# The last key's term as one product per output half, its values laid out in memory, and a projection in halves and passes

## The chip, the core and the metric

One NeuronCore of one Trainium2 chip. The metric is the device time of one execution in microseconds (us), the median over the runs shown. The profile is of one execution of its own.

## The reference

Sizes: x 64 x 32 x 512, context 64 x 257 x 512, 16 heads; weights as in the shapes below. Everything is float32.

```python
x = x + cross(layernorm(x), ctx)      # layernorm again with gamma, beta inside
    q = (xn @ w_q) -> 16 heads of 64;  k, v = split(ctx @ w_kv)
    attn = softmax(q * 64**-0.5 @ k.T)          # 32 queries x 257 keys
    out = ((attn @ v) @ w_out + b_out) * tanh(gate)
x = x + linear_attention(layernorm(x))          # W_Q, W_K, W_V
x = x + ffn(layernorm(x))                       # silu(gate) * up, hidden 1536
```

## The kernel before

Five engines run programs written out by hand, tied by semaphores: `wait_ge` holds the engine, `then_inc` counts. A value in float32 is kept for PE as a rounded high part and the rest (fp32r), and `three` multiplies high by high, low by high, high by low (L83 to L85). Some products are plain float32.

**Projection** (`project_queries`). Four blocks of 512 tokens, t = 0 to 3. DVE normalises twice (`norm_moments`, `norm_scale`), each time asking GpSimd (POOL) for a power; PE turns the result (L300), DVE applies gamma and beta (`affine`), ACT rounds it (`high_x`), DVE subtracts (`split_x`). PE forms eight outputs j of four chunks c, twelve products each. The weights come as eight pieces into a ring of six (`WeightSplit`): ACT rounds (L110), POOL subtracts (L230), and a slot is loaded again after that. ACT takes all eight pieces before `high_x`.

**Cross-attention** (`cross_attention`). 16 turns of four batches; the last turn is written apart. q is folded with the key weights once a turn (`fold_pair`, `low_fold`), so keys and values are the context itself. For batch b, PE forms four score tiles of 257 keys, DVE takes the maximum, ACT the exponential, POOL scales, DVE turns 32x32 blocks, SP's four DMAs exchange them between partitions (`exchange`), ACT and DVE split them (`high_probs`, `split_probs`), and PE multiplies with 256 of the context's rows in four chunks (`mix_chunk`), copied by DVE (`keep_mix`, L718). `out_half` multiplies the mix with the value weights: eight heads a half, two 64-column products of 128 columns at a time in plain float32 (L634). The 257th key is apart: its values v for all batches are computed once (`last_values`, ACT L930, a scratch array, `v_dram`) and loaded each turn into 16 rows of `last_v`; its weights go from `last_z` by a transpose and a product with a mask `own` into `last_p` (`keep_last`, L730 and L733), and one product per head adds the term (L641). ACT and DVE split each half (`high_out`, `low_out`), SP stores it. In the loop eight fold products and four score tiles of the next turn stand between the halves, in the last turn nothing.

Before the loop PE folds, scores batch 0 and computes v; SP waits for `v_stored` ahead of the loop's first turn.

## Time and profile before

| | |
|---|---|
| median of 3 runs | 1829.09 us (1827.91 to 1829.17) |
| profiled execution | 1831.52 us; span 1829.7 us, granted clock 0.994 |
| busy: PE, DVE, ACT, POOL | 98%, 60%, 36%, 30% |
| a turn of the loop | 62.9 us, 15 of them and the last |

A row of a timeline gives start, duration, engine, line, operation, out<-in, count, and in brackets the idle time before and what ended it. PE rows start when the one ahead is still draining: count from start to start. The granted clock is a share of 2.4 GHz, so 0.50 is 1.2 GHz.

### The profile page before, as it was taken

To read this page: it belongs to the slowest core of one execution; us is meant where nothing else is said; L and a number is where in the kernel's file an instruction comes from. 1 tells how busy PE (TensorE), PEld (TensorE's weight loads), DVE (VectorE), ACT (ScalarE), POOL (GpSimd) and SP (SyncE) were. 2 spreads that over 40 slices of the span, in tenths; PEclk is the share of its full clock that TensorE was granted. 3 is DMA by queue.
4 is the path that set the end of the run, shared out by engine and by line. 5 is a ranking of instruction groups with operands and counts; after the bars stand their busy time and mean duration, and the time that the engine had idled before them with its cause. 6 is when DMAs were issued, how large, how long until landed. Compare 5 with 4: busy or idle time off the path is not lost.

```text
span 1829.7 us, 38379 instructions
## 1 busy us (share of the span) xinstructions
PE 1794.3 (98%) x14608; PEld 1545.7 (84%) x14608; DVE 1104.6 (60%) x2271; ACT 666.8 (36%) x1356; POOL 557.9 (30%) x546
## 2 busy tenths in 40 slices
PE   5999999999999999999999999999999999999999
PEld 4888988998898899889988987788887878888887
DVE  6636566666756665666667566787888643333322
ACT  2245444545544454445445444311112411111111
POOL 3015434534444354345344444421121000000000
PEclk9999999999999999999999999999999999999999
DMA  7325444543554454445435538523440501010100
GB/s 254 127 97 145 123 109 125 139 133 90 146 137 116 114 150 123 107 127 140 133 90 145 137 105 237 160 78 96 126 139 13 180 6 69 1 69 0 46 1 23
DMA packets 236124, 199.23 MB, mean 109 GB/s; under 512 B 12896, under 2 KB 193376, under 8 KB 236064
## 3 DMA queue, kind: packets, MB, share of 16 engines
q1 hardware_dynamic: 231632, 189.74, 36.6%
q10 hardware_dynamic: 4432, 8.65, 1.3%
q8 instruction: 42, 0.69, 0.2%
q14 instruction: 18, 0.15, 0.0%
HBM read 130.98 MB, written 33.82 MB: 90 GB/s over the span
## 4 chain that ended last, share of the span: by engine, by line
PE 90%; DMA 1%; DVE 1%; SPq 0%; POOL 0%; issue 0%; ACT 0%; DVEq 0%; POOLq 0%; ACTq 0%
PE s_ps L83 25%; PE s_ps L84 24%; PE s_ps L85 24%; PE s_ps L579 7%; PE s_ps L634 6%; PE s_ps L641 1%; PE s_ps L1373 1%; PE s_ps L1387 1%; PE s_ps L1313 0%; PE s_ps L1398 0%; DMA a_xin<-x 0%; DMA a_m_xn<-x 0%; PE s_ps L588 0%; PE s_ps L1362 0%; DMA o_lo<-x_o_lo 0%
## 5 line engine op out<-in xcount | busy, mean ns | idle before, releaser
L83 PE MATMUL s_ps<-w_cT_hi,w_space_hi 128*128 128x258 f32 x1024 | 293.3, 286 | 0.2 <-DVE w_space_lo L725 0.2
L84 PE MATMUL s_ps<-w_cT_lo,w_space_hi 128*128 128x258 f32 x1024 | 289.9, 283 | 0.0
L85 PE MATMUL s_ps<-w_cT_hi,w_space_lo 128*128 128x258 f32 x1024 | 288.3, 282 | 0.0
L530 POOL TENSOR_TENSOR x_prob<-x_prob,x_share 128x256 f32<-128x256 f32 x256 | 156.0, 615 | 337.8 <-DVE x_share L692 329.9
L718 DVE COPY x_mix<-s_ps 128x512 f32<-128x512 f32 x256 | 174.5, 687 | 69.4 <-PE s_ps L85 67.0
L83 PE MATMUL s_ps<-x_pT_hi,x_cn_hi 128*128 128x512 f32 x512 | 206.3, 403 | 4.1 <-DVE x_mix L718 4.1
L850 ACT ACTIVATE x_prob<-s_ps,x_negmax 128x257 f32<-128x257 f32 x256 | 121.9, 476 | 240.9 <-DVE x_negmax L687 237.7
L85 PE MATMUL s_ps<-x_pT_hi,x_cn_lo 128*128 128x512 f32 x512 | 201.6, 394 | 0.0
L84 PE MATMUL s_ps<-x_pT_lo,x_cn_hi 128*128 128x512 f32 x512 | 200.9, 392 | 0.0
L83 PEld LDWEIGHTS s_ps<-w_cT_hi,w_space_hi 128*128 128x128 f32 x1024 | 193.4, 189 | 6.2 <-issue 3.8
L84 PEld LDWEIGHTS s_ps<-w_cT_lo,w_space_hi 128*128 128x128 f32 x1024 | 193.9, 189 | 0.7
L85 PEld LDWEIGHTS s_ps<-w_cT_hi,w_space_lo 128*128 128x128 f32 x1024 | 192.9, 188 | 0.0
L687 DVE TENSOR_REDUCE x_negmax<-s_ps 128x1 f32<-128x257 f32 x256 | 106.9, 418 | 125.2 <-PE s_ps L85 125.1
L725 DVE TENSOR_TENSOR w_space_lo<-s_ps,w_space_hi 128x512 fp32r<-128x512 f32 x256 | 160.4, 679 | 33.0 <-ACT w_space_hi L863 33.0
L519 POOL TENSOR_TENSOR w_cT_lo<-e_raw_T,w_cT_hi 128x1028 fp32r<-128x1028 f32 x64 | 141.5, 2211 | 126.9 <-ACT w_cT_hi L835 126.9
L524 POOL TENSOR_TENSOR x_cn_lo<-e_raw_n,x_cn_hi 128x1024 fp32r<-128x1024 f32 x64 | 153.0, 2391 | 73.8 <-ACT x_cn_hi L841 73.8
L863 ACT ACTIVATE w_space_hi<-s_ps 128x512 fp32r<-128x512 f32 x256 | 130.5, 615 | 33.0 <-PE s_ps L579 33.0
L634 PE MATMUL s_ps<-x_mix,e_wv 128*64 128x128 f32 x2048 | 138.3, 275 | 0.0
L579 PEld LDWEIGHTS s_ps<-e_q,e_wk 64*128 64x128 f32 x2048 | 118.1, 188 | 15.7 <-issue 13.3
L579 PE MATMUL s_ps<-e_q,e_wk 64*128 64x128 f32 x2048 | 127.2, 277 | 1.7 <-SPq L495 1.7
L634 PEld LDWEIGHTS s_ps<-x_mix,e_wv 128*64 128x64 f32 x2048 | 114.2, 137 | 11.3 <-DVE x_mix L718 8.9
L83 PEld LDWEIGHTS s_ps<-x_pT_hi,x_cn_hi 128*128 128x128 f32 x512 | 96.8, 189 | 26.9 <-issue 4.8
(204 smaller groups left out, 3504.7 us busy)
## 6 DMA issues: line engine op xcount, KB each, us to landing
e_raw_T<-ctx_T SPq DMA_DIRECT2D x64, 514.0 KB, 4.7
e_raw_n<-ctx_nat SPq DMA_DIRECT2D x64, 512.0 KB, 4.1
x_prob_T<-x_blocks SPq DMA_DIRECT2D x256, 128.0 KB, 2.7
q<-q_q ACTq DMA_DIRECT2D x16, 512.0 KB, 2.8
e_q<-q SPq DMA_DIRECT2D x16, 512.0 KB, 4.1
o_hi<-x_o_hi SPq DMA_DIRECT2D x32, 256.0 KB, 3.3
o_lo<-x_o_lo SPq DMA_DIRECT2D x32, 256.0 KB, 3.8
a_oT_hi<-o_hi SPq DMA_DIRECT2D x16, 512.0 KB, 4.3
```

What stands on the lines that cost most here:

```text
L83: pe.matmul(out, lhs[0], rhs[0], start=start, stop=False)
L84: pe.matmul(out, lhs[0], rhs[1], start=False, stop=False)
L85: return pe.matmul(out, lhs[1], rhs[0], start=False, stop=stop)
L519: pool.tensor_tensor(cT[b % 2][1][:, :, 0:SK], raw_T[:, :, :], f32(cT[b % 2][0][:, :, 0:SK]), ALU.subtract).then_inc(Tlo_done.sem, 1)
L524: pool.tensor_tensor(cn[b % 2][1][:, :, :], raw_n[:, :, :], f32(cn[b % 2][0][:, :, :]), ALU.subtract).then_inc(nlo_done.sem, 1)
L530: pool.tensor_tensor(prob[:, i, 0:KT * P], prob[:, i, 0:KT * P], share[:, i:i + 1].to_broadcast([P, KT * P]), ALU.mult)\
L579: mm = pe.matmul(ps[:, banks[h], c * P:(c + 1) * P], wk[r, j, c * P:(c + 1) * P], q[r, j, :], start=True, stop=True)
L634: pe.matmul(out[h], w_v[:, c, n * HE:(n + 1) * HE], mix[:, c, :, place(n)], start=c == 0, stop=False)
L718: dve.tensor_copy(mix[:, c, b, :], ps[:, M_BANK[c % 2], :]).then_inc(mix_kept.sem, 1)
L725: dve.tensor_tensor(lo, ps[:, fold_order(ahead, j)[0][h], :].rearrange("p (c n) -> p c n", n=SQ), f32(hi), ALU.subtract).then_inc(fold_lo. ...
L850: act.activation(prob[:, i, 0:SK], ps[:, S_BANK[i], 0:SK], ACT.Exp, bias=negmax[:, i:i + 1], accum_out=total[:, i:i + 1]).then_inc(exp_don ...
L863: act.activation(of_head(fold[0], 2 * j + h), ps[:, fold_order(ahead, j)[0][h], :].rearrange("p (c n) -> p c n", n=SQ), ACT.Copy)\
```

## The change

- **The last key.** Each row of the last key's weights and values is split in high and low; three columns (high, low, minus the high part's copy) are made for each batch and key. `last_rows`, a new input, is the mask: 16 columns of which row belongs to which column block, and one of signs. Each half has one 128x128 by 512 product in fp32r (L711 in the numbering of the change) ahead of its 64-column ones, with a spread of its own (`spread_last`); the second is made behind `low_out` of the first half.
- **The values.** ACT writes the rounded v twice, DVE makes the rest, ACT writes it; SP first fills `v_laid` with zeros from `last_v`, and then lays v out by eight DMAs of 16x24x64 (`spread_v`) and waits. A turn then loads 128x256 with one DMA in place of four.
- **The projection.** The norm goes in two halves of two tiles. The first block's first four outputs are formed in three passes: high by high, low weights, low x. ACT rounds x straight from PSUM. Five products of zeros (`WARM`) run at the start. The second block is turned ahead of j = 7, not 5. POOL splits one piece of weights between the norms, not two, and the rest after both halves.

On PE, in `out_half(0)` of the loop, before:

```order
L634 MATMUL s_ps<-x_mix,e_wv 64x128 [waits x_mix_kept]
L634 MATMUL s_ps<-x_mix,e_wv 64x128
L634 MATMUL s_ps<-x_mix,e_wv 64x128 [waits x_mix_kept]
L634 MATMUL s_ps<-x_mix,e_wv 64x128
L634 MATMUL s_ps<-x_mix,e_wv 64x128 [waits x_mix_kept]
L634 MATMUL s_ps<-x_mix,e_wv 64x128
L634 MATMUL s_ps<-x_mix,e_wv 64x128 [waits x_mix_kept]
L634 MATMUL s_ps<-x_mix,e_wv 64x128
L637 ISA
L638 REGISTER_ALU [waits x_v_loaded]
L641 MATMUL s_ps<-x_last_p,x_last_v 64x128 [waits x_last_kept]
L641 MATMUL s_ps<-x_last_p,x_last_v 64x128
```

and now:

```order
L709 REGISTER_ALU [waits x_v_loaded]
L710 REGISTER_ALU [waits x_mix_kept]
L711 MATMUL s_ps<-x_last_p,x_last_v 128x512 [waits x_last_kept]
L720 MATMUL s_ps<-x_mix,e_wv 64x128 x6
L720 MATMUL s_ps<-x_mix,e_wv 64x128 [waits x_mix_kept]
L720 MATMUL s_ps<-x_mix,e_wv 64x128 x25
```

The L641 products behind each block of eight are gone, and one of 512 columns stands ahead, with the waits for the values and the third chunk in front of it.

On DVE, from the third batch's last copy to the fold's fourth pair, before (`last_t` to `last_p` is `keep_last`), and now:

```order
L718 COPY x_mix<-s_ps 128x512 [waits x_mixed] x2
L730 STREAM_TRANSPOSE x_last_t<-x_last_z 128x128 [waits x_last_ready]
L732 ISA [waits x_last_turned]
L733 TENSOR_TENSOR x_last_p<-x_last_t,x_own 128x512 [waits x_o_ready]
L725 TENSOR_TENSOR w_space_lo<-s_ps,w_space_hi 128x16x32 [waits x_fold_hi]
L725 TENSOR_TENSOR w_space_lo<-s_ps,w_space_hi 128x16x32 [waits x_fold_hi]
L718 COPY x_mix<-s_ps 128x512 [waits x_mixed] x2
```

```order
L797 COPY x_mix<-s_ps 128x512 [waits x_mixed] x2
L809 STREAM_TRANSPOSE x_last_t<-x_last_z 128x64 [waits x_last_ready]
L812 CAST x_last_h<-x_last_t 128x64 [waits x_last_turned]
L814 SCALAR_TENSOR_TENSOR x_last_t<-x_last_t,x_own,x_last_h 128x64 [waits x_last_turned]
L817 ISA [waits x_last_turned]
L822 TENSOR_TENSOR x_last_p<-x_last_t,x_own 128x512 [waits x_o_ready]
L804 TENSOR_TENSOR w_space_lo<-s_ps,w_space_hi 128x16x32 [waits x_fold_hi]
```

Two operations and two waits came in. In the same turn, behind `low_out` (L829) and ahead of `low_fold(6)`, the second spread now stands:

```order
L829 TENSOR_TENSOR x_o_lo<-s_ps,x_o_hi 128x512 [waits x_o_hi_done]
L822 TENSOR_TENSOR x_last_p<-x_last_t,x_own 128x512
L802 REGISTER_ALU
L804 TENSOR_TENSOR w_space_lo<-s_ps,w_space_hi 128x16x32 [waits x_fold_hi]
L802 REGISTER_ALU
L804 TENSOR_TENSOR w_space_lo<-s_ps,w_space_hi 128x16x32 [waits x_fold_hi]
```

On POOL, at the start of the projection, before and now (L222 and L232 are the powers, L230 and L225 the split of weights):

```order
L222 TENSOR_TENSOR q_rstd<-q_shifted,q_power 128x4 [waits q_var_ready,q_power_set]
L230 TENSOR_TENSOR q_wq_lo<-q_raw,q_wq_hi 128x512 [waits q_w_hi_done,q_dve_chain]
L230 TENSOR_TENSOR q_wq_lo<-q_raw,q_wq_hi 128x512 [waits q_w_hi_done]
L222 TENSOR_TENSOR q_rstd<-q_shifted,q_power 128x4 [waits q_var_ready]
L230 TENSOR_TENSOR q_wq_lo<-q_raw,q_wq_hi 128x512 [waits q_w_hi_done,q_normed]
L230 TENSOR_TENSOR q_wq_lo<-q_raw,q_wq_hi 128x512 [waits q_w_hi_done] x5
```

```order
L232 TENSOR_TENSOR q_rstd<-q_shifted,q_power 128x2 [waits q_var_ready,q_power_set]
L232 TENSOR_TENSOR q_rstd<-q_shifted,q_power 128x2 [waits q_var_ready]
L225 TENSOR_TENSOR q_wq_lo<-q_raw,q_wq_hi 128x512 [waits q_w_hi_done]
L232 TENSOR_TENSOR q_rstd<-q_shifted,q_power 128x2 [waits q_var_ready] x2
L225 TENSOR_TENSOR q_wq_lo<-q_raw,q_wq_hi 128x512 [waits q_w_hi_done,q_normed]
L225 TENSOR_TENSOR q_wq_lo<-q_raw,q_wq_hi 128x512 [waits q_w_hi_done] x6
```

The second piece moved behind the powers and the wait for the norm.

The core of the diff:

```diff
+            def low_weights(numbers):
+                for n in numbers:
+                    pool.wait_ge(weights.hi_done, n + 1)
+                    pool.tensor_tensor(pieces[n][2], weights.raw[n % weights.RING][:, :], f32(pieces[n][1]),
+                                       ALU.subtract).then_inc(weights.lo_done, 1)
+
             for t in range(TURNS):
                 for k in range(2):
-                    pool.wait_ge(var_ready.sem, var_ready.at(t, k + 1))
-                    pool.tensor_tensor(rstd[:, :], shifted[:, :], power[:, :], ALU.pow).then_inc(rstd_done.sem, 1)
+                    for h, half in enumerate(HALVES):
+                        pool.wait_ge(var_ready.sem, var_ready.at(t, 2 * k + h + 1))
+                        pool.tensor_tensor(rstd[:, half], shifted[:, half], power[:, half], ALU.pow)\
+                            .then_inc(rstd_done.sem, 1)
                     if t == 0:
-                        if k == 0:
-                            pool.wait_ge(dve_chain, SCALED)
-                        else:
-                            pool.wait_ge(normed.sem, normed.at(0, 1))
-                        for n in range(2) if k == 0 else range(2, len(pieces)):
-                            pool.wait_ge(weights.hi_done, n + 1)
-                            pool.tensor_tensor(pieces[n][2], weights.raw[n % weights.RING][:, :], f32(pieces[n][1]),
-                                               ALU.subtract).then_inc(weights.lo_done, 1)
+                        if k == 1:
+                            pool.wait_ge(normed.sem, normed.at(0, 2))
+                        low_weights(range(1) if k == 0 else range(1, len(pieces)))
...
                     dve.wait_ge(x_loaded.sem, x_loaded.at(t, 16))
-                norm_moments(dve, chain, xin, stats, moments, shifted, TT, var_ready,
-                             x_first if t == 0 else None)
-                dve.wait_ge(rstd_done.sem, rstd_done.at(t, 1))
-                chain.step(norm_scale(dve, xn, xin, moments, rstd, TT))
-                norm_moments(dve, chain, xn, stats, moments, shifted, TT, var_ready)
-                dve.wait_ge(rstd_done.sem, rstd_done.at(t, 2))
-                norm_scale(dve, xn2, xn, moments, rstd, TT).then_inc(normed.sem, 1)
+                for half in HALVES:
+                    spread(xin, half)
+                for h, half in enumerate(HALVES):
+                    chain.step(scale(xn, xin, half, h + 1))
+                    spread(xn, half)
+                for h, half in enumerate(HALVES):
+                    scale(xn2, xn, half, h + 3).then_inc(normed.sem, 1)
...
                 for c in range(DC):
-                    act.wait_ge(affine_done.sem, affine_done.at(t, c + 1))
-                    act.activation(xT[t % 2][0][:, c, :], affine[:, c, :], ACT.Copy).then_inc(xhi_done.sem, 1)
-
+                    act.wait_ge(turned.sem, turned.at(t, c + 1))
+                    act.activation(xT[t % 2][0][:, c, :], ps[:, c, :], ACT.Identity, scale=g[:, c:c + 1],
+                                   bias=b[:, c:c + 1]).then_inc(xhi_done.sem, 1)
+
+            act.wait_ge(once, 48)
...
+            def first_products():
+
+                for part in range(2):
+                    for c in range(DC):
+                        if part == 0:
+                            pe.wait_ge(weights.hi_done, c + 1)
+                            pe.wait_ge(xhi_done.sem, xhi_done.at(0, c + 1))
+                        else:
+                            pe.wait_ge(weights.lo_done, c + 1)
+                        for j in range(4):
+                            pe.matmul(ps[:, 4 + j, :], wt[part][:, c, j * P:(j + 1) * P], xT[0][0][:, c, :],
+                                      start=part == 0 and c == 0, stop=False)
+                for j in range(4):
+                    for c in range(DC):
+                        if j == 0:
+                            pe.wait_ge(xlo_done.sem, xlo_done.at(0, c + 1))
+                        mm = pe.matmul(ps[:, 4 + j, :], wt[0][:, c, j * P:(j + 1) * P], xT[0][1][:, c, :],
+                                       start=False, stop=c == DC - 1)
+                    mm.then_inc(q_ready.sem, 1)
+
+            pe.wait_ge(zeroed, 1)
+            pe.wait_ge(var_ready.sem, var_ready.at(0, 2))
+            for _ in range(WARM):
+                pe.matmul(ps[:, 7, :], q[:, 0, 0:P], q[:, 0, :], start=True, stop=True)
             pe.wait_ge(once, 48)
-            turn_x(0)
+            turn_first()
+            first_products()
...
-    last_p = s.sb("last_p", [P, TILES, GB, SQ])
-    last_v = s.sb("last_v", [P, inner])
-    last_z, last_t = s.sb("last_z", [P, TILES, SQ]), s.sb("last_t", [P, TILES, SQ])
-    own = s.sb("own", [P, GB])
+    last_p = s.sb("last_p", [P, 2, PAIRS // 2, GB, SQ], F32R)
+    last_v = s.sb("last_v", [P, 2, P], F32R)
+    last_z, last_t = s.sb("last_z", [P, TILES, SQ // 2]), s.sb("last_t", [P, 2, SQ])
+    last_h = s.sb("last_h", [P, 2, SQ], F32R)
+    OWN = GB * PAIRS // 2
+    own = s.sb("own", [P, OWN + 1])
...
         def load_v(t):
             sp.wait_ge(o_ready.sem, o_ready.at(t, 0))
+            sp.dma_start(f32(last_v[:, :, :]), v_laid[bass.ds(t, 1), :, :].rearrange("t p (m n) -> p (t m) n", m=2))\
+                .then_inc(v_loaded.sem, 16)
+
+        def spread_v():
+
+            sp.wait_ge(v_cleared, 16)
+            sp.wait_ge(v_stored, 48)
+            src = v_dram.rearrange("(t b) k (m l g e) -> t (b k) m l g e", t=TURNS, m=2, l=2, g=HT)
+            dst = v_laid.rearrange("t p (m h e) -> t p m h e", m=2, h=2)
             for g in range(HT):
-                dst = last_v[g * SQ:g * SQ + GB, :].rearrange("b (i g e) -> b i g e", g=HT, e=HE)[:, :, g, :]
-                src = v_dram[bass.ds(t * GB, GB), :].rearrange("b (i g e) -> b i g e", g=HT, e=HE)[:, :, g, :]
-                sp.dma_start(dst, src).then_inc(v_loaded.sem, 16)
+                for l in range(2):
+                    at = g * SQ + l * SQ // 2
+                    sp.dma_start(dst[:, at:at + GB * PARTS, :, g % 2, :], src[:, :, :, l, g, :]).then_inc(v_spread, 16)
...
+        sp.dma_start(own[:, :], last_rows).then_inc(own_loaded, 16)
         sp.wait_ge(cleared, 1)
+        sp.dma_start(v_laid.rearrange("t p n -> p t n"),
+                     f32(last_v[:, :, :]).rearrange("p (t m) n -> p t (m n)", t=1).to_broadcast([P, TURNS, 2 * P]))\
+            .then_inc(v_cleared, 16)
...
-        sp.wait_ge(v_stored, 16)
+        spread_v()
+        sp.wait_ge(v_spread, 16 * 2 * HT)
...
-            pool.tensor_tensor(last_z[:, :, b % GB], prob[:, :, SK - 1], share[:, :], ALU.mult)\
+            at = b % GB * PARTS
+            pool.tensor_tensor(last_z[:, :, at:at + PARTS], prob[:, :, SK - 1:SK].to_broadcast([P, TILES, PARTS]),
+                               share[:, :].rearrange("p (i k) -> p i k", k=1).to_broadcast([P, TILES, PARTS]), ALU.mult)\
...
         def out_half(t, m):
+            if m == 0:
+                pe.wait_ge(v_loaded.sem, v_loaded.at(t, 16))
+                pe.wait_ge(mix_kept.sem, mix_kept.at(t, GB * DC - 1))
+            pe.wait_ge(last_kept.sem, last_kept.at(t, m + 1))
+            pe.matmul(ps[:, O_BANK[m], :], last_v[:, m, :], last_p[:, m, :, :, :].rearrange("p j b q -> p (j b q)"),
+                      start=True, stop=False)
             for j in range(4 * m, 4 * m + 4):
                 out = [ps[h * HE:(h + 1) * HE, O_BANK[m], j % 4 * P:(j % 4 + 1) * P] for h in range(2)]
                 for c in range(DC):
-                    if j == 0:
-                        pe.wait_ge(mix_kept.sem, mix_kept.at(t, (GB - 1) * DC + max(c + 1, DC - 1)))
+                    if j == 0 and c == DC - 1:
+                        pe.wait_ge(mix_kept.sem, mix_kept.at(t, GB * DC))
                     for h in range(2):
                         n = 2 * j + h
-                        pe.matmul(out[h], w_v[:, c, n * HE:(n + 1) * HE], mix[:, c, :, place(n)],
-                                  start=c == 0, stop=False)
-                if j == 0:
-                    pe.wait_ge(v_loaded.sem, v_loaded.at(t, 16 * HT))
-                    pe.wait_ge(last_kept.sem, last_kept.at(t, 1))
-                for h in range(2):
-                    n = 2 * j + h
-                    mm = pe.matmul(out[h], last_v[:, n * HE:(n + 1) * HE],
-                                   last_p[:, n // HT, :, :].rearrange("p b q -> p (b q)"), start=False, stop=True)
+                        mm = pe.matmul(out[h], w_v[:, c, n * HE:(n + 1) * HE], mix[:, c, :, place(n)],
+                                       start=False, stop=j == 4 * m + 3 and c == DC - 1)
...
         def keep_last(t):
             dve.wait_ge(last_ready.sem, last_ready.at(t, GB))
-            dve.transpose(last_t[:, :, :], last_z[:, :, :]).then_inc(last_turned.sem, 1)
+            dve.transpose(last_t[:, :, :], last_z[:, :, :].rearrange("p (m l) r -> p m (l r)", m=2))\
+                .then_inc(last_turned.sem, 1)
             dve.wait_ge(last_turned.sem, last_turned.at(t, 1))
+            dve.tensor_copy(last_h[:, :, :], last_t[:, :, :]).then_inc(last_turned.sem, 1)
+            dve.wait_ge(last_turned.sem, last_turned.at(t, 2))
+            dve.scalar_tensor_tensor(last_t[:, :, :], last_t[:, :, :], own[:, OWN:OWN + 1], f32(last_h[:, :, :]), ALU.mult,
+                                     ALU.add).then_inc(last_turned.sem, 1)
+            dve.wait_ge(last_turned.sem, last_turned.at(t, 3))
             dve.wait_ge(o_ready.sem, o_ready.at(t, 0))
-            dve.tensor_tensor(last_p[:, :, :, :],
-                              last_t[:, :, :].rearrange("p i (b q) -> p i b q", b=1).to_broadcast([P, TILES, GB, SQ]),
-                              own[:, :].rearrange("p (i b q) -> p i b q", i=1, q=1).to_broadcast([P, TILES, GB, SQ]),
+            spread_last(t, 0)
+
+        def spread_last(t, m):
+            shape = [P, OWN, SQ]
+            dve.tensor_tensor(last_p[:, m, :, :, :].rearrange("p j b q -> p (j b) q"),
+                              last_t[:, m, :].rearrange("p (x q) -> p x q", x=1).to_broadcast(shape),
+                              own[:, 0:OWN].rearrange("p (x q) -> p x q", q=1).to_broadcast(shape),
                               ALU.mult).then_inc(last_kept.sem, 1)
...
             low_out(t, 0)
+            spread_last(t, 1)
...
+        dve.wait_ge(own_loaded, 16)
+        dve.wait_ge(v_rounded, 1)
+        dve.tensor_tensor(all_last[1], ps[0:B, M_BANK[0]:M_BANK[0] + 2, :], f32(all_last[0]), ALU.subtract)\
+            .then_inc(v_copied, 1)
...
-        act.activation(all_last, ps[0:B, M_BANK[0]:M_BANK[0] + 2, :], ACT.Copy).then_inc(v_copied, 1)
+        act.activation(all_last[0], ps[0:B, M_BANK[0]:M_BANK[0] + 2, :], ACT.Copy).then_inc(v_rounded, 1)
+        act.wait_ge(v_rounded, 1)
+        for k in (0, 2):
+            act.dma_start(v_dram[:, k, :].rearrange("b (h n) -> b h n", h=2), f32(all_last[0])).then_inc(v_stored, 16)
         act.wait_ge(v_copied, 1)
-        act.dma_start(v_dram.rearrange("b (h n) -> b h n", h=2), all_last).then_inc(v_stored, 16)
+        act.dma_start(v_dram[:, 1, :].rearrange("b (h n) -> b h n", h=2), f32(all_last[1])).then_inc(v_stored, 16)
...
+    last_rows = np.zeros((4, 2, 16, 17), np.float32)
+    for g, l, b, k in itertools.product(range(4), range(2), range(4), range(3)):
+        last_rows[g, l, 3 * b + k, 4 * (2 * l + g // 2) + b] = -1 if k == 2 else 1
+        last_rows[g, l, 3 * b + k, 16] = -1 if k == 2 else 0
```

## Rows read from the trace of the kernel before

**Rows 1.** Busy shares on the page, part 1.

```profile
PE 1794.3 (98%) x14608; PEld 1545.7 (84%) x14608; DVE 1104.6 (60%) x2271; ACT 666.8 (36%) x1356; POOL 557.9 (30%) x546
```

**Rows 2.** PE timeline, output halves of two turns (start, us, engine, line, operation, count).

```profile
250.88 1.29 PE L634 MATMUL s_ps<-x_mix,e_wv 128*64 128x128 f32 x16
...
313.18 0.39 PE L84 MATMUL s_ps<-x_pT_lo,x_cn_hi 128*128 128x512 f32 x1
313.41 0.40 PE L85 MATMUL s_ps<-x_pT_hi,x_cn_lo 128*128 128x512 f32 x1
313.74 1.29 PE L634 MATMUL s_ps<-x_mix,e_wv 128*64 128x128 f32 x16
...
318.45 1.27 PE L579 MATMUL s_ps<-e_q,e_wk 64*128 64x128 f32 x18
...
326.37 1.09 PE L634 MATMUL s_ps<-x_mix,e_wv 128*64 128x128 f32 x16
327.30 0.39 PE L641 MATMUL s_ps<-x_last_p,x_last_v 128*64 128x128 f32 x4
327.51 1.04 PE L634 MATMUL s_ps<-x_mix,e_wv 128*64 128x128 f32 x16
...
330.89 0.39 PE L83 MATMUL s_ps<-w_cT_hi,w_space_hi 128*128 128x258 f32 x1
```

**Rows 3.** Weight loads (PEld) in the timeline of the first half.

```profile
314.59 0.20 PEld L634 LDWEIGHTS s_ps<-x_mix,e_wv 128*64 128x64 f32 x4 [0.22 <-DVE x_mix L718]
```

**Rows 4.** DVE timeline: a turn of the loop, and the last turn.

```profile
306.71 0.30 DVE L730 STREAM_TRANSPOSE x_last_t<-x_last_z 128x128 f32<-128x128 f32 x1
307.14 0.69 DVE L733 TENSOR_TENSOR x_last_p<-x_last_t,x_own 128x512 f32<-128x512 f32 x1
...
309.72 0.69 DVE L718 COPY x_mix<-s_ps 128x512 f32<-128x512 f32 x1 [0.69 <-PE s_ps L85]
...
320.29 2.48 DVE L725 TENSOR_TENSOR w_space_lo<-s_ps,w_space_hi 128x512 fp32r<-128x512 f32 x4 [0.40 <-ACT w_space_hi L863]
...
1124.51 1.47 DVE L733 TENSOR_TENSOR x_last_p<-x_last_t,x_own 128x512 f32<-128x512 f32 x1
```

**Rows 5.** Chain of waits behind the last turn's first half (start, us, what).

```profile
1136.95 0.61 ACT x_o_hi L877
```

**Rows 6.** Timeline of the loop's first turn: SP, ACT and PE.

```profile
146.91 3.35 SPq L435 DMA_DIRECT2D x_last_v<-v  x4
...
152.87 3.08 SPq L423 DMA_DIRECT2D x_prob_T<-x_blocks  x4
...
158.21 1.15 ACT L858 ACTIVATE x_pT_hi<-x_prob_T 128x512 fp32r<-128x512 f32 x2 [0.41 <-DMA x_prob_T<-x_blocks]
160.53 0.48 ACT L850 ACTIVATE x_prob<-s_ps,x_negmax 128x257 f32<-128x257 f32 x1 [1.17 <-DVE x_negmax L687]
...
162.32 0.28 PE L83 MATMUL s_ps<-w_cT_hi,w_space_hi 128*128 128x258 f32 x1
```

**Rows 7.** PE timeline of the last turn, around its longest idle time.

```profile
1123.76 0.76 PE L83 MATMUL s_ps<-x_pT_hi,x_cn_hi 128*128 128x512 f32 x1 [4.13 <-DVE x_mix L718]
...
1129.44 0.44 PE L84 MATMUL s_ps<-x_pT_lo,x_cn_hi 128*128 128x512 f32 x1
```

**Rows 8.** Stretch of 1127 to 1129 us (PE busy, granted clock, DMA share, GB/s).

```profile
1127.00:1129.00 2.00, 2.00 (x6) 0.50 0.04 16
```

**Rows 9.** Timeline of the projection's start: POOL, DVE, ACT and PE.

```profile
11.23 2.49 POOL L230 TENSOR_TENSOR q_wq_lo<-q_raw,q_wq_hi 128x512 fp32r<-128x512 f32 x2 [2.03 <-DVE q_xn L141]
...
15.40 1.91 DVE L141 TENSOR_SCALAR q_xn<-q_xn,q_moments,q_rstd 128x512 f32<-128x512 f32 x4 [1.13 <-POOL q_rstd L222]
16.74 0.63 ACT L110 ACTIVATE q_wq_hi<-q_raw 128x512 fp32r<-128x512 f32 x1 [1.12 <-DMA q_raw<-wq]
...
23.06 0.47 PE L83 MATMUL q_ps<-q_xT_hi,q_wq_hi 128*128 128x512 f32 x1 [2.32 <-DVE q_xT_lo L255]
...
42.33 0.48 PE L83 MATMUL q_ps<-q_xT_hi,q_wq_hi 128*128 128x512 f32 x1
```

93 lines of the change are left out of this document (61 added, 32 removed).

## The prediction

> **What bounds the kernel.** I read the page's busy shares first, then the PE timeline of one turn of the cross-attention loop, then what stands beside it. PE is busy for 98% of the span [rows 1]. Busy is a modelled number, so what I trust is the distance between starts: inside a turn one matmul starts after another with no gap that a release explains. A product of the 512-wide fp32r kind starts 0.23 us after the one ahead of it, and the output's second half runs 4.52 us from its first start at 326.37 to the next tile's at 330.89 [rows 2]. So a turn's length is the sum of PE's own starts, and instructions taken from PE there shorten the kernel as long as DVE, ACT, POOL and SP keep their lead. The time of a difference is made against the profiled execution: span 1829.7 us, 1831.52 us as timed; the median of the runs shown is 1829.09 us, 2.4 us under it. What a measurement of this kernel can tell from no change is about 0.2%, 3.7 us.
>
> **Part 1, the last key's product, steady turns.** Each half of the output holds four blocks of L641, x4 records each. One block takes 0.21 us, from 327.30 to the next start at 327.51 [rows 2]; by the half's 80 records in 4.52 us it would be 0.226. I take 0.22, so 0.87 us a half. In its place comes one product of 128x128 weights and 512 columns, fp32r, the kind with the pitch of 0.23. The second half so saves 0.87 - 0.23 = 0.64 us. The first half is longer today: 313.74 to 318.45 [rows 2], 4.71 against 4.52. The difference of 0.2 is a wait: PE's weight load stands idle for 0.22 us until DVE has copied the last mix chunk [rows 3]. The new product is put ahead of that wait and covers it. But it waits itself for the third chunk's copy, so its weights can't be loaded early, for which I add 0.1 us. The first half: 0.87 + 0.20 - 0.23 - 0.10 = 0.74. A turn saves 1.38 us; bounds are 0.92 (the product at twice its pitch in both halves) and 1.65 (no load delay, the block at 0.226, the product wholly inside the wait). Fifteen turns of the loop: **20.7 us**, 14 to 25.
>
> DVE's additions. In keep_last the transpose starts at 306.71, takes 0.30, and 0.13 later, at 307.14, the spread starts [rows 4]. Two operations of 64 columns come in between, each with such a wait behind it; the nearest row is that transpose of 128 columns, 0.43 with its wait. I take 0.24 apiece for the half width, 0.48 us. DVE is idle for 0.69 us before the copy at 309.72 [rows 4], which is the cover; with it gone each microsecond would reach the next mix chunk. The second spread (0.69 us, as L733 today) stands between low_out and low_fold 6, where DVE idles 0.40 us at 320.29 [rows 4]: it makes the low parts of the fold 0.29 late. PE needs the last of them for the third score tile, more than a microsecond behind. Nothing is charged, and this is rival C. POOL's last_z with three columns a key and the single load of last_v (SP issues one for four) have cover too: they are 0.2 us of POOL, and SP then waits for DVE's tiles anyway.
>
> **Part 2, the last turn.** There no fold and no scores stand between the halves, so PE's second half has to wait for the second spread, which DVE does behind ACT's high_out and its own low_out. ACT's copy is 0.61 [rows 5]; low_out is taken to cost what the spread does, 0.69 [rows 4], and the spread the same; with hand-overs 2.0 us from the first half's end, where now the second half follows at once. The halves themselves get shorter by 0.74 and 0.64, less 0.1 for the second's weight load. A loss of 2.0 - 0.74 - 0.54 = **0.7 us**, up to 1.5 if the spread meets POOL's weight work, where L733 once took 1.47 [rows 4]. The chain of waits behind it (POOL and DVE split weights) isn't shortened by what PE does.
>
> **Part 3, laying the values out, before the loop.** Today ACT writes v once, and SP is released by its landing at 146.91 [rows 6]. Now a third write follows, of what DVE leaves: DVE takes the rounded part off 64x1024 values in PSUM. Twice the 0.69 of a 512-wide operation is the upper end, 0.69 the lower; I take 1.2, so the third write lands at 148.1. Only then does SP issue eight scattered DMAs and wait for all of them, with the exchange of key block 1 queued behind. No row shows such a DMA. Nearest are the exchange's four: 3.08 us to issue, and the last landed when ACT was released at 158.21, 2.3 us behind the last issue [rows 6]. Eight at 0.77 and 2.3 make 8.4 us; if packets count (3072 rows against 1024), three times 3.08 and 2.3 make 11.5. I take 9.4, near the first because the queue was busy with issuing: spread at 157.5. With load_v and load_q ahead, the exchange starts at 158.6 instead of 152.87, 5.7 late. ACT's high_probs blocks the exps of block 2 behind it: today the third is over at 161.0 and PE needs it for the tile at 162.3 [rows 6], a lead of 1.3 us. PE stands for 5.7 - 1.3 = 4.4 us. A stand of that length has a second price: after 4.13 us idle in the last turn, thirteen matmuls took 5.68 us (0.44 each) [rows 7] with a granted clock of 0.50 [rows 8], the 1.2 GHz level, 2.7 us more than at 0.23. Together **7.1 us lost**; 0 if the spread lands by 151, 14 if it needs twice as long.
>
> The Trainium skill, page "DMA: Bandwidth & Descriptors", section Specifications, asks for at least 512 B a transfer, below which the engine reads, modifies and writes. The spread's rows are 256 B, so by that rule these DMAs would be the slower bound or worse, and the loss some 9 to 10 us; no row of this trace prices such a row alone.
>
> The zeroing of the laid-out array (2 MB) goes ahead of the loads of the keys. I charge nothing for it, and no row prices it: a load of keys that comes 3 us later delays only the first normalisation, whose tiles PE uses after the scores of a whole block.
>
> **Part 4, the projection.** The first matmul starts at 23.06 [rows 9], long after the transposes. What gates it now is the eighth piece of weights: ACT rounds all eight before it touches x, and the ring of six lets piece 8 load only when POOL has split two. Today POOL splits both at 11.23 to 13.72, between two norms, and ACT rounds the eighth at 16.74, 3.0 later [rows 9]. Held back, the second split stands behind both halves' norm. The norm itself ends at 17.3 now (15.40 + 1.91); with halves the waits for POOL's power are filled, 1.1 to 1.2 us each; I take 15.8. POOL splits by 17.1, the piece lands at 20.1, ACT is done with it at 20.8, x rounded straight from PSUM is there at 21.4. **So the matmuls start 1.7 us sooner, not more.** From there PE has 96 of them and one set of transposes: 96 x 0.227 + 1.9, plus the low clock for 2.7, ends at 47.8. Before: j 5 to 7 start at 42.33 [rows 9], and 36 x 0.227 end at 50.5. The gain is **2.7 us**; the passes need the low parts only at the 33rd matmul, so POOL and DVE, which share time there, are out of the way. Bounds: 0 (a wait for the second block of tokens, whose norm starts some 2.4 later than now), and 5.4 (the clock stays up, since five products of zeros run ahead).
>
> **Sum:** 20.7 - 0.7 - 7.1 + 2.7 = 15.6 us. Against its own time the profiled execution would be 1831.52 - 15.6 = 1815.9; from the median, 1829.09 - 15.6 = **1813.5 us**.
>
> **Rivals.**
> A, the spread is hidden: it lands while PE does blocks 0 and 1 and no stand of PE forms. For it: SP waits for DVE's tiles until 152.87. Against it: eight issues alone end at 154. It gives 15.6 + 7.1 = 22.7, 1806.4 us.
> B, the change doesn't do what it says: the new product costs what the old ones did. For it: the old blocks are two 64-column products side by side, and joining them fills rows with zeros, so no work need be saved. If it took 0.87, only the wait of 0.2 is won, 3.0 us, less 5.1 of the other parts: 1831.2, no change. Against it: products of the same types and size run at 0.23 [rows 2].
> C, DVE's extra 1.2 us a turn reach PE through the exchange of the next turn: 0.4 us a turn would be 6 us, 1819.5 us. Against it: 0.69 and 0.40 of idle time just there [rows 4].
> D, slower: SP is held by the spread. With X us from the third write's landing to the spread's, PE stands for X - 5.0, and has 22.7 to spare with 2.7 of them for the clock: the kernel is slower from X = 25 on, which is 130 ns a row on each of 16 engines, where the exchange's 1024 packets in 5.3 us [rows 6] make 83 with the latency in. At X = 35 it is 30 + 2.7 - 22.7 = 10 us slower, 1839.1 us. Rows of 256 B from memory to memory speak for it, the size of the factor against it.
>
> **Chances.** Forecast 0.60, A 0.17, C 0.14, B 0.04, D 0.03, else 0.02. The range takes in the forecast's bounds, A and most of C: 1804 to 1821 us. Faster by more than 0.2%: 0.92; within: 0.04; slower: 0.04.
>
> **What would show it.** Right: the distance from one turn's first half to the next, 62.86 us now (250.88 to 313.74) [rows 2], becomes 61.5; one idle row of PE of 4 to 5 us near 160, with the granted clock at 0.50 behind it; the first fp32r product near 21.4; PE idle for 2 us between the halves of the last turn. Wrong: turns of 62.5 or more (B or C, told apart by the new product's own distance), an idle time before the loop over 10 us, or none.

## The result and the profile after

The changed kernel takes 1818.53 us (median of 5 runs, 1817.80 to 1821.15), the kernel before 1829.09. The ratio is 0.9947, 95% interval [0.9936, 0.9958]: **faster by 10.6 us**, 8 to 12 by the interval. The forecast was 1813.5, 15.6 faster, with a range of 1804 to 1821. The sign and the range held, a third of the gain did not come.

The profiled execution took 1818.93 us with a span of 1817.1, so it lies 0.4 us over its median, where the one before lay 2.4 over. The spans therefore differ by 12.6 us, 2.0 more than the medians. The page's busy shares after, to be read beside [rows 1]:

```profile
PE 1781.1 (98%) x14138; PEld 1526.1 (84%) x14138; DVE 1120.5 (62%) x2336; ACT 669.3 (37%) x1356; POOL 561.2 (31%) x555
```

PE has 470 matmuls fewer and DVE 65 operations more. What a busy share can't say, the distances between fixed points on PE can. I cut the span at five places that both kernels have: the first fold of q (L579, now L659); the fold behind turn 0's first half; the same fold of turn 14; the first product of the heads (`a_oT_hi`); the end.

| stretch, us | before | after | difference | forecast |
|---|---|---|---|---|
| start to the first fold | 121.22 | 117.99 | -3.2 | -2.7 |
| to the fold in turn 0 | 71.50 | 78.02 | +6.5 | +6.4 |
| 14 turns | 880.15 | 861.94 | -18.2 | -19.3 |
| to the heads (last turn) | 68.33 | 73.36 | **+5.0** | +0.1 |
| to the end | 688.50 | 685.79 | -2.7 | 0 |

The forecast's column is made of its terms: turn 0 is 7.1 less 0.74 for its own first half, the fourteen turns are 14 x 1.38, the last stretch before the heads is 0.7 less the 0.64 of turn 14's second half. Of the last stretch, -2.7, PE's idle time explains 1.3: before, PE waited 0.92 us there for rows (`a_xin`) and 0.42 for `f_h_lo`, and after the change it waits for neither; the rest is not explained. In the profiles of all experiments below but one (x3) this stretch takes 685.5 to 687.3.

The column "after" is one profile. Profiles of the experiments that leave a place as in the change show how far it moves: the first fold at 118.0 to 119.4, turn 0's stretch 78.0 to 79.3, a turn 61.57 to 61.58, the stretch to the heads 72.0 to 73.9.

**A turn.** PE timeline, the two halves of the turn that [rows 2] shows of before:

```profile
314.80 0.40 PE L85 MATMUL s_ps<-x_pT_hi,x_cn_lo 128*128 128x512 f32 x1
315.09 0.49 PE L711 MATMUL s_ps<-x_last_p,x_last_v 128*128 128x512 f32 x1
315.51 3.71 PE L720 MATMUL s_ps<-x_mix,e_wv 128*64 128x128 f32 x64
319.15 2.06 PE L659 MATMUL s_ps<-e_q,e_wk 64*128 64x128 f32 x32
...
327.01 0.40 PE L711 MATMUL s_ps<-x_last_p,x_last_v 128*128 128x512 f32 x1
327.34 3.71 PE L720 MATMUL s_ps<-x_mix,e_wv 128*64 128x128 f32 x64
330.98 0.39 PE L83 MATMUL s_ps<-w_cT_hi,w_space_hi 128*128 128x258 f32 x1
```

Half 0 runs from 315.09 to 319.15, 4.06 us where it took 4.71; half 1 from 327.01 to 330.98, 3.97 where it took 4.52. The new product stands 0.42 and 0.33 us ahead of what follows it, not 0.33 and 0.23. With the 0.1 us that both starts come nearer to what is ahead of them, a turn is 1.30 us shorter (61.57 against 62.87).

What the new product multiplies is, for each batch and key, the weights' parts high, high, low with the values' parts high, low, high. The low part of the weights is made as high minus value and gets its sign from the mask's -1 (L814 and L822); it is not a copy of the high part.

**Turn 0.** Chain of waits, from the copy of v to the exchange that follows:

```profile
141.58 5.66 DMA v<-x_mix
147.33 0.62 SPq L510
...
151.96 2.77 DMA v_laid<-v
155.08 0.36 SPq L498
...
156.48 0.66 SPq L489
```

The third write of v lands 5.66 us after ACT issues it; then eight issues, 5.24 us in all; then 2.4 us to the release at 155; then the exchange. PE behind it, and a stretch of 2 us with its granted clock (columns: PE, PEld, DVE, ACT, POOL busy, clock, DMA share, GB/s):

```profile
164.74 0.58 PE L83 MATMUL s_ps<-w_cT_hi,w_space_hi 128*128 128x258 f32 x1 [5.01 <-ACT x_prob L943]
```
```profile
166.00:168.00 2.00, 2.00 (x12) 2.00 (x12) 1.51 (x5) 1.49 (x5) 2.00 (x3) 0.56 0.02 4
```

That is the stand that was forecast, 5.0 us for 4.4, with the clock at 0.5, the 1.2 GHz level, behind it for some 3 us: the first thirteen products take 3.0 us, where such a product takes 0.12 at full clock, so the low clock costs some 1.4 us.

**The last turn.** PE's and DVE's timelines, beside [rows 7] and the last row of [rows 4]:

```profile
1117.13 0.47 PE L711 MATMUL s_ps<-x_last_p,x_last_v 128*128 128x512 f32 x1
1117.53 3.81 PE L720 MATMUL s_ps<-x_mix,e_wv 128*64 128x128 f32 x64
1124.45 0.79 PE L711 MATMUL s_ps<-x_last_p,x_last_v 128*128 128x512 f32 x1 [3.11 <-DVE x_last_p L822]
1125.17 6.21 PE L720 MATMUL s_ps<-x_mix,e_wv 128*64 128x128 f32 x64
1131.31 0.50 PE L83 MATMUL s_ps<-w_cT_hi,a_oT_hi 128*128 128x512 f32 x1
```
```profile
1109.00 1.05 DVE L812 CAST x_last_h<-x_last_t 128x64 fp32r<-128x64 f32 x1
1110.09 1.24 DVE L814 SCALAR_TENSOR_TENSOR x_last_t<-x_last_t,x_own,x_last_h 128x64 f32<-128x64 f32 x1
...
1122.02 0.69 DVE L829 TENSOR_TENSOR x_o_lo<-s_ps,x_o_hi 128x512 fp32r<-128x512 f32 x1 [3.19 <-ACT x_o_hi L970]
1122.62 1.77 DVE L822 TENSOR_TENSOR x_last_p<-x_last_t,x_own 128x512 fp32r<-128x512 f32 x1
```
```profile
1125.00:1129.00 4.00, 4.00 (x37) 3.83 (x38) 2.27 (x3) 0.20 (x1) 0.52 (x1) 0.50 1.01 331
```

Here is the missing gain. PE stands for 3.1 us, and the second half then takes 6.86 us (1124.45 to 1131.31), where one takes 3.97 in the loop: the granted clock is 0.50 until 1129 and 0.67 on average from there to 1131. From the first half to the heads it was 9.1 us; now it is 14.2.

The stand is 3.11 us in every profile with this order, the time at the low clock behind it is not always as long. In five profiles (the change, x2, x3, x4, x7) it is 14.1 to 14.4 us from the first half to the heads, in four (x6, x9, z1, z3) 12.9 to 13.1. In x6 the second half takes 5.54 us (1120.12 to 1125.66), since the clock comes back sooner (columns as above):

```profile
1122.00:1124.00 2.00, 2.00 (x28) 2.00 (x26) 0.95 (x2) 0.00 (x0) 0.00 (x0) 0.68 0.99 368
```

**The projection.** Before the first product PE and ACT did this:

```profile
14.17 2.15 PE L338 MATMUL q_ps<-q_ident,q_xn 128*128 128x128 f32 x16 [0.37 <-DVE q_xn L260]
21.19 5.42 PE L352 MATMUL q_ps<-q_xT_hi,q_wq_hi 128*128 128x512 f32 x16 [4.88 <-ACT q_xT_hi L299]
```
```profile
19.75 0.63 ACT L110 ACTIVATE q_wq_hi<-q_raw 128x512 fp32r<-128x512 f32 x1 [5.93 <-DMA q_raw<-wq]
20.29 2.77 ACT L299 ACTIVATE q_xT_hi<-q_ps,q_beta,q_gamma 128x512 fp32r<-128x512 f32 x4
```

The last piece of weights holds ACT until 19.75, and PE stands for 4.9 us although x was turned at 16.3.

### The profile page after: what moved, and what is told of

It is laid out like the page before. It is cut to its first block, busy times and chain, and to the rows that moved or that the text cites. A ratio compares the mean times of both kernels' runs of the same rounds, so it can differ in the third digit from the quotient of the medians.

```text
span 1817.1 us, 37412 instructions
## 1 busy us (share of the span) xinstructions
PE 1781.1 (98%) x14138; PEld 1526.1 (84%) x14138; DVE 1120.5 (62%) x2336; ACT 669.3 (37%) x1356; POOL 561.2 (31%) x555
## 4 chain that ended last, share of the span: by engine, by line
PE 90%; DVE 1%; DMA 1%; SPq 1%; ACT 0%; issue 0%; DVEq 0%; ACTq 0%
PE s_ps L83 25%; PE s_ps L84 24%; PE s_ps L85 24%; PE s_ps L659 7%; PE s_ps L720 7%; PE s_ps L1469 1%; PE s_ps L1483 1%; PE s_ps L711 1%; PE s_ps L1409 0%; PE s_ps L1494 0%; PE s_ps L668 0%; PE s_ps L1458 0%; DMA x_prob_T<-x_blocks 0%; DMA v<-x_mix 0%; SPq L510 0%
## 5 line engine op out<-in xcount | busy, mean ns | idle before, releaser
L602 POOL TENSOR_TENSOR x_cn_lo<-e_raw_n,x_cn_hi 128x1024 fp32r<-128x1024 f32 x64 | 153.0, 2390 | 73.9 <-ACT x_cn_hi L934 73.9
L659 PEld LDWEIGHTS s_ps<-e_q,e_wk 64*128 64x128 f32 x2048 | 118.1, 188 | 15.7 <-issue 13.3
L659 PE MATMUL s_ps<-e_q,e_wk 64*128 64x128 f32 x2048 | 127.2, 277 | 1.7 <-SPq L570 1.7
L720 PE MATMUL s_ps<-x_mix,e_wv 128*64 128x128 f32 x2048 | 121.4, 278 | 0.0
```

The lines of the kernel that those rows point to most:

```text
L602: pool.tensor_tensor(cn[b % 2][1][:, :, :], raw_n[:, :, :], f32(cn[b % 2][0][:, :, :]), ALU.subtract).then_inc(nlo_done.sem, 1)
L659: mm = pe.matmul(ps[:, banks[h], c * P:(c + 1) * P], wk[r, j, c * P:(c + 1) * P], q[r, j, :], start=True, stop=True)
L720: mm = pe.matmul(out[h], w_v[:, c, n * HE:(n + 1) * HE], mix[:, c, :, place(n)], start=False, stop=j == 4 * m + 3 and c == DC - 1)
```

## Experiments

All were compared with the kernel before in the same sessions; its medians there were 1827.7 to 1830.8. The changed kernel was not run again beside them, so a difference "from the change" compares medians of different sessions, and the 3 us by which the kernel before moved may be in it; the ratios to the kernel before are free of that. The stretches are those of the table above, each of one profile.

**x1: the last turn's second spread, sooner.**

```diff
             if more:
                 low_fold(t, 1, 5)
+            else:
+                spread_last(t, 1)
             low_out(t, 0)
-            spread_last(t, 1)
             if more:
+                spread_last(t, 1)
```

> In the last turn alone the second spread stands ahead of low_out of the first half, behind the last chunk's copy, where DVE was idle for 3.2 us in the trace of the change. Theory (the last turn's second spread is what the forecast undersized): PE's idle 3.1 us between the halves goes, and with it the second half's slow run (6.14 us for its 64 products against 3.77 in the first half, and 0.4 in the product ahead), so the head stage starts about 6 us sooner and the kernel takes 5 to 6 us less than the change, 1812.5 to 1813.5. Rival (weights bound the stage behind): the halves close up, PE then waits as long for weights or rows in the head stage, and the time moves by under 1.5 us. Second rival (the slow run has nothing to do with the gap): 3 us less, with the second half still at 6 us.

Measured: 1816.93 us, ratio 0.9937 [0.9921, 0.9954]; span 1813.4. The stretch to the heads is 67.35 us, 6.0 less than in the change. PE and DVE:

```profile
1117.85 0.47 PE L711 MATMUL s_ps<-x_last_p,x_last_v 128*128 128x512 f32 x1
1118.25 3.81 PE L720 MATMUL s_ps<-x_mix,e_wv 128*64 128x128 f32 x64
1121.99 0.50 PE L711 MATMUL s_ps<-x_last_p,x_last_v 128*128 128x512 f32 x1
...
1126.06 0.50 PE L83 MATMUL s_ps<-w_cT_hi,a_oT_hi 128*128 128x512 f32 x1
```
```profile
1119.46 0.68 DVE L822 TENSOR_TENSOR x_last_p<-x_last_t,x_own 128x512 fp32r<-128x512 f32 x1
```

The stand and the slow half are gone together: 8.2 us from the first half to the heads, for 14.2. So in the change's profile the 3.1 us of waiting cost 6.0, and 4.7 to 4.9 in those where the clock came back sooner. The stretch behind the heads' start is 1.5 us longer (PE now waits 1.5 us for rows, `a_xin`), so the span fell by 3.7. The 5 to 6 us expected of the whole did not come: the median fell by 1.6, by the ratios 1.8 with some 3.5 either way. The four runs are 1815.2, 1815.6, 1818.3 and 1818.4, the profile is of the first, and no other shows where the last two lose. The mechanism is shown by the stretch, its price in the whole is not; z5 below bears on it.

**x2 and z1: turn 0.** x2 writes SP's first turn apart:

```diff
+            if first:
+                spread_v()
             exchange(t, 3)
+            if first:
+                sp.wait_ge(v_spread, 16 * 2 * HT)
+                load_v(t)
```

> SP's turn 0 is written apart: the eight DMAs that lay v out are issued between the load behind exchange 2 and exchange 3 (7 us in which SP was idle in the trace of the change), and load_v follows exchange 3. Theory (the wait for v_stored and the spread ahead of exchange 1 cost turn 0 all of its 7.2 us): PE's idle row of 5.0 us near 160 goes, no stretch at a granted clock of 0.5 behind it, and the time is 6.5 to 7.5 us under the change, about 1811.5. Rival (the turn is late for another reason too, the third write of v, for which DVE's first mix copy waits until 147.3): some 1 to 3 us stay, 1813 to 1816. Second rival (the spread just moves the stand to exchange 3): the same time as the change.

Measured: 1814.53 us, 0.9917 [0.9901, 0.9934]. The stand near 160 is gone, but turn 0's stretch is 74.99, 3.0 less instead of 7: the first rival, with 4 us left where it had 1 to 3. Chain of waits and PE in x2:

```profile
142.27 7.76 DMA v<-x_mix
150.14 0.70 DVE x_mix L802
```
```profile
150.89 0.50 PE L83 MATMUL s_ps<-x_pT_hi,x_cn_hi 128*128 128x512 f32 x1 [2.27 <-DVE x_mix L802]
```
```profile
152.00:154.00 2.00, 2.00 (x7) 1.57 (x6) 1.46 (x4) 0.00 (x0) 1.07 (x1) 0.54 0.00 0
```

The third write lands 7.8 us after its issue here, with the next q's load now sent at 141.0 beside it (whether that load delays it was not tested), and DVE may not overwrite its source before. The gate had been there in the change too, hidden behind the SP's (DVE's copy at 147.35 ended a wait for that DMA, of 0.50 us). Of the twelve products behind the 2.27 us, seven ran at 0.43 and five at full speed, 1.4 us more. z1 gives that write a semaphore of its own:

```diff
-            dve.wait_ge(v_stored, 48)
+            dve.wait_ge(v_stored, 32)
...
+            dve.wait_ge(v_low_stored, 16)
             keep_mix(t, 2, 0)
```

> As x2_spread_later, and the third write of v counts on a semaphore of its own: DVE's first mix copy, which overwrites what the first two writes read, waits for those two alone, and the copies of the third batch, which overwrite what the third reads, for the third. In x2 PE stood 2.3 us behind that copy and then ran twelve products at 0.43 us. Theory (that wait is all that was left of turn 0's loss): the distance from the first fold to turn 0's first fold behind the half, 75.0 us in x2 and 78.0 in the change, becomes 70.8 to 71.2 (71.5 before, less 0.7 of the half), and the time is about 7 us under the change, 1811.5. Rival (the first two writes land as late, or the exchange is late through traffic): 73 us or more, 1814.

Measured: 1812.94 us, 0.9903 [0.9888, 0.9919]; turn 0's stretch is 71.04. The theory holds: all 7.0 us of turn 0's loss were these two gates, the spread ahead of exchange 1 and the copy behind the third write.

**x9: sixteen DMAs for the same rows.**

```diff
-                    sp.dma_start(dst[:, at:at + GB * PARTS, :, g % 2, :], src[:, :, :, l, g, :]).then_inc(v_spread, 16)
+                    for m in range(2):
+                        sp.dma_start(dst[:, at:at + GB * PARTS, m:m + 1, g % 2, :], src[:, :, m:m + 1, l, g, :])\
+                            .then_inc(v_spread, 16)
```

> The same rows are laid out by sixteen DMAs instead of eight, each half as large. Theory (issuing on SP, 0.65 us a DMA, is the larger part of the spread's hold, with 2.4 to 2.8 us of landing behind the last): eight more issues, 5.2 us more, PE's stand grows from 5.0 to 10.2 us and the kernel by 5 to 5.5, to 1823.8. Rival (the rows' transfer holds it): landing takes as long in all, and the time does not move.

Measured: 1824.63 us (10 runs), 0.9977 [0.9967, 0.9986], 6.1 more than the change. SP's timeline, where the change has 5.24 for eight:

```profile
148.35 10.32 SPq L511 DMA_DIRECT2D v_laid<-v  x16
160.59 0.37 SPq L498 DMA_DIRECT2D x_last_v<-v_laid  x1
```

5.1 us more to issue, landing no later behind the last, turn 0's stretch 5.9 longer, PE's stand 9.7 us. The number of DMAs sets the price of issuing, 0.65 us each with half the rows as with all. The Trainium skill, page "DMA: Bandwidth & Descriptors", section Specifications, asks for 512 B a transfer; the rows of 256 B were not what held the queue here, and the loss of 9 to 10 us that the forecast worked out by that rule did not come.

**x6 and x4: the projection.** x6 lets POOL split two pieces between the norms, as before the change:

```diff
-                        low_weights(range(1) if k == 0 else range(1, len(pieces)))
+                        low_weights(range(2) if k == 0 else range(2, len(pieces)))
```

> POOL splits two pieces of weights between the norms, as before the change, instead of one. Theory of the forecast (the eighth piece, which can load only when two are split, gates the first product at 21.2): the piece comes 1 us or more sooner, ACT reaches x sooner, and the first product starts 1 to 2.5 us sooner; the time falls by up to 2 us. Rival (DVE's norm is held by POOL's powers behind the second split and by the port that they share): the norm ends 1.2 us or more later, and the first product starts no sooner; the time is the same or up to 1 us more.

Measured: 1815.32 us, 0.9929 [0.9912, 0.9945]; the first fold starts at 113.65, 4.3 us sooner. PE and ACT in x6:

```profile
15.49 2.14 PE L338 MATMUL q_ps<-q_ident,q_xn 128*128 128x128 f32 x16 [1.90 <-DVE q_xn L260]
18.00 3.91 PE L352 MATMUL q_ps<-q_xT_hi,q_wq_hi 128*128 128x512 f32 x16 [0.37 <-ACT q_xT_hi L299]
```
```profile
15.10 0.63 ACT L110 ACTIVATE q_wq_hi<-q_raw 128x512 fp32r<-128x512 f32 x1 [1.16 <-DMA q_raw<-wq]
```

Both the theory and the rival are seen: the norm's end moves from 15.2 to 16.5, and the piece comes 4.65 us sooner. The piece wins, and by more than the theory had: the first product starts 3.2 us sooner, not 1 to 2.5. The first sixteen products then take 3.75 us (18.00 to 21.75), not 5.26, as PE had stood for 0.37 us and not 4.88. Holding POOL back cost the change 4.3 us by this pair of profiles, more than the whole new projection brought. By averages it is 5.4: the three profiles with two early pieces (x6, z2, z5) have the first fold at 113.1 to 113.7, the seven with one at 118.7.

x4 puts eight products of zeros behind the transposes, none ahead of them:

```diff
             pe.wait_ge(once, 48)
             turn_first()
+            for _ in range(WARM):
+                pe.matmul(ps[:, 7, :], q[:, 0, 0:P], q[:, 0, :], start=True, stop=True)
```

> Eight products of zeros stand behind the transposes of the first block instead of five ahead of them, so PE works through most of the 4.9 us until the first real product. Theory (an idle PE before 21.2 is why the first real products run with a granted clock of 0.50): the first 16 take 3.6 to 3.9 us instead of 5.3, and the time is 1.3 to 1.6 us under the change. Rival (zeros keep nothing up, or the copies of x gate the products anyway): no difference. What is given back: up to 0.5 us if the zeros run past 21.2.

Measured: 1822.78 us, 0.9968 [0.9955, 0.9980], 4.2 slower than the change; the first fold at 119.91.

```profile
14.28 3.65 PE L338 MATMUL q_ps<-q_ident,q_xn 128*128 128x128 f32 x16 [14.28 <-DVE q_xn L260]
17.72 7.15 PE L366 MATMUL q_ps<-q_q 128*128 128x512 f32 x16
24.30 4.24 PE L352 MATMUL q_ps<-q_xT_hi,q_wq_hi 128*128 128x512 f32 x16
```

A miss by its size. The zeros took 6.6 us, so the real products began 3.1 us late; the transposes, with nothing ahead of them, took 3.4. But the first sixteen real products took 4.08 us instead of 5.26 at a granted clock of 1.00: with a busy PE ahead of them the clock was up. The mechanism stands, this way of using it does not pay. Two things stay open. The transposes' 3.4 us, for 2.15 behind the zeros of the change, have a granted clock of 1.00 beside them in the trace too. And the first fold is only 1.9 us later than in the change's profile; another 1.3 of the 4.2 is in turn 0's stretch (79.31).

**x7 and x8: the new product in a turn.** x7 changes the place of `low_fold(t, 1, 4)` from behind the second copy to behind the third (`c == 1` to `c == 2`).

> In the loop DVE copies the third chunk of the last key block's mix ahead of low_fold(4), not behind it. In the trace of the change that copy starts at 314.28, at once behind low_fold(4) (313.09), though PE had the chunk ready before, and the new product of the first half waits for it: its weights load at 315.08 after 0.32 us idle. Theory (that copy, not the product, sets the first half's start): the first product starts 0.2 to 0.3 us sooner a turn, 3 to 4.5 us in fifteen turns, 1814 to 1815.5. Rival (the fourth chunk's copy is then as late and PE waits for that): no difference. Second rival (low_fold 4 and 5 come late for the fold behind the half): slower by some tenths of a us a turn.

Measured: 1822.84 us, 0.9966 [0.9954, 0.9979], and turns of 61.80 instead of 61.57, 3.4 us in fifteen. The theory falls. The weights of the new product now load without a gap, but the wait moves one chunk on, as the first rival had it, and is longer there: half 0 takes 4.35 us for 4.07. The loss is of the second rival's size, by another way than the fold behind the half. PE's weight loads in x7:

```profile
317.39 0.19 PEld L711 LDWEIGHTS s_ps<-x_last_p,x_last_v 128*128 128x128 f32 x1
...
318.99 2.82 PEld L720 LDWEIGHTS s_ps<-x_mix,e_wv 128*64 128x64 f32 x52 [0.41 <-DVE x_mix L797]
```

x8 leaves the product out.

> The product of the last key is left out of both halves (the output lacks the last key's term); all its waits, DVE's work and the loads stay. It prices the product. Theory (in the second half it costs its pitch and the switch behind it, 0.33 us from its start to the next; in the first half it covers the wait for the fourth chunk's copy, so its 0.42 is mostly hidden): a turn shorter by 0.33 to 0.55 us, 5 to 8.5 us in all. Rival (both cost what stands between the starts): 0.75 a turn, 11.5 to 12 us. Rival B of the forecast (the new product costs as much as the old blocks): over 0.87 a half.

Measured: 1812.89 us, 0.9912 [0.9895, 0.9928]; a turn is 61.12 us, 0.45 less than the change's 61.57. Half 1 takes 3.64, so the product costs 0.33 there. Half 0 takes 3.84 (256.29 to 260.13), 0.22 less than 4.06, for behind the missing product a wait comes up:

```profile
257.14 2.82 PEld L718 LDWEIGHTS s_ps<-x_mix,e_wv 128*64 128x64 f32 x52 [0.22 <-DVE x_mix L795]
```

So the two products cost a turn 0.45 us: 0.55 in the halves, less the 0.1 by which both halves start nearer to what is ahead of them. In half 0 about half of the product's 0.42 hides the wait for the fourth chunk's copy, as the forecast had it. Rival B would need 0.87 a half.

**x3 and z3: the old projection.** x3 is the change with `project_queries` of before.

> The change with the projection of before. By the two traces the projection brought 3.2 us (the first fold at 117.99 against 121.22), so this takes 3.2 us more than the change, 1821.7; the forecast's term was 2.7. Rival (the gain is given back later, where transfers gate the start of the cross-attention): under 1 us more.

Measured: 1833.95 us, 1.0030 [1.0017, 1.0043], 15.4 more than the change. The first fold starts at 119.92, turn 0's stretch is 78.77 (0.7 more), the turns are the change's (61.58), but from the heads to the end it took 697.7 us, 11.9 more. Two rows of PE there:

```profile
1244.37 1.11 PE L1346 MATMUL s_ps<-s_ident,a_xn 128*128 128x128 f32 x4 [5.06 <-issue]
...
1250.01 0.80 PE L84 MATMUL s_ps<-w_cT_lo,a_oT_hi 128*128 128x512 f32 x1 [4.11 <-issue]
```

Nothing released them. The page of x3 counts 50 packets on the queue named instruction, where before and the change have 42. z3 adds 47 repeats of a wait that is over, to PE's program:

```diff
-            pe.wait_ge(once, 48)
+            for _ in range(48):
+                pe.wait_ge(once, 48)
             turn_x(0)
```

> As x3_old_projection, with one wait of PE that is already over written 48 times at the start, where PE stands for 17 us anyway. x3 was 15 us slower than the change, of which its fold's start explains 2; its head stage took 12 us more, with two idle rows of PE of 5.1 and 4.1 us that end in no release, near 1244 and 1250. Theory (they hang on where PE's instructions lie in its program): with 48 instructions more the rows go or move elsewhere, and the time changes by several us, down to about 1821. Rival (the old projection causes them, by data or traffic): the same rows at the same place, 1834.

Measured: 1822.33 us, 0.9959 [0.9944, 0.9974]. The rows are gone, the stretch is 685.8, and the queue's row reads as in the change:

```profile
q8 instruction: 50, 0.82, 0.2%
```
```profile
q8 instruction: 42, 0.69, 0.2%
```

(x3 above, z3 below.) So x3's total is no price of the projection. z3's median is 3.8 us over the change's, but the kernel before took 1830.8 there, 1.7 more than in the change's session: by the ratios, 0.9959 against 0.9947, it is 2.2 us, with some 3.5 either way. The traces agree with the smaller figure: the first fold is at 119.9 to 121.2 in the three profiles with the old projection (120.5 on average) and at 118.0 to 119.4 in the seven with the new one and one early piece, x4 aside (118.7): 1.8 us.

**z2 and z5: what gains, together.** z2 joins x1, z1 and x6, and moves the load of the next q behind exchange 3 in turn 0.

> All four edits that gained on the change: the last turn's second spread ahead of low_out (6.0 us between the last turn and the heads), the spread of v behind exchange 2, the third write apart (7 us in turn 0), and two pieces split between the norms (4.3 us at the first fold). The load of turn 1's q moves behind exchange 3 too. If they add up: 17 us, less 1.5 us that the head stage gives back in waits for rows (seen in x1), so 1802 to 1804 us; each place's distance as in its own experiment. Rival (they meet at one bound, weights or rows at the head stage): 1806 or more, with idle rows of PE between 1100 and 1150.

Measured: 1815.53 us, 0.9919 [0.9905, 0.9932], a miss by 12 us. The edits add up in the first and last stretches (first fold 113.05, to the heads 67.48), but the moved load spoils turn 0, 83.88 us:

```profile
173.09 5.49 PE L667 MATMUL s_ps<-e_q,e_wk 64*128 64x128 f32 x48 [9.68 <-DMA e_q<-q]
```

z5 takes that move back.

> z2_best with the load of turn 1's q back where the change has it, ahead of exchange 1. In z2 that load was issued at 168.6 and PE stood 9.7 us for it at turn 1's first fold. Theory (that stand was the only thing in the way, and the four edits add up): the distance from the first fold to turn 0's fold behind the half is 71.0 again (83.9 in z2), no idle row of PE for q, and the time is 1802 to 1804 us. Rival (with the fold 5 us sooner, another load or the low half of the values is late in turn 0): 73 us or more and 1805 to 1808.

Measured: **1802.70 us** (1801.55 to 1803.99), 0.9861 [0.9845, 0.9878]; span 1800.9, granted clock 0.998. Its stretches are 113.20, 71.44, 862.04, 67.50 and 686.7 us. PE:

```profile
17.42 3.91 PE L352 MATMUL q_ps<-q_xT_hi,q_wq_hi 128*128 128x512 f32 x16 [0.37 <-ACT q_xT_hi L299]
...
1110.11 0.50 PE L717 MATMUL s_ps<-x_last_p,x_last_v 128*128 128x512 f32 x1
```

25 us faster than the kernel before and 16 faster than the change, of which x1 brings 5.9, z1 6.6 and x6 4.8 by its stretches; the stretch behind the heads' start gives back 0.9. The theory holds, with the 1802 to 1804 that it named. It is also the better evidence for x1's gain: by their own medians x1, z1 and x6 would have brought 10, by their ratios 13.

## Why the prediction was right, and where it was off

**Part 1, the turns (20.7 forecast): right, 1.30 a turn for 1.38.** 0.65 + 0.55 for the halves and 0.1 for the starts. The product's own distance was undersized by 0.1 us a half (0.33 and 0.42, against the pitch of 0.23 and that plus 0.1), the cover in half 0 is shown by x8. The 0.1 charged for a late weight load is real: 0.32 us of idle time ahead of the load, and a start 0.30 behind the product ahead of it instead of 0.23. x7 shows that nothing is to be had by moving the copy. The upper bound of 1.65 a turn is not what its terms give: four blocks at 0.226 in each half, less one pitch of 0.23, are 1.58.

**Part 2, the last turn (0.7 forecast, 1.5 at most): wrong, this is the step that failed.** It cost 5.1 us from the half to the heads in the change's profile, and 3.8 to 4.0 in the four where the clock came back sooner. The gap forecast at 2.0 us became 3.1, since DVE took 1.77 us for the spread while POOL split weights, not 0.69; that was named, as the upper bound. What was not priced is the low clock behind the gap: "a stand of that length has a second price" was said of 4.4 us in Part 3 and not asked of 2.0 here, where it was put at nothing without a reason; x2 shows 1.4 us behind a gap of 2.27. With it 3.1 us of waiting became 6.0 here, as x1 shows. The two added DVE operations ran 1.05 and 1.24 us here against 0.20 and 0.28 in the loop, beside the same work of POOL, and the first half came some 0.5 us later: it starts 8.8 us behind the end of PE's idle time of 4.2 us (1108.32), before the change 8.35 (1123.76).

**Part 3, turn 0 (7.1 forecast): right, 7.0 to 7.2, in part by luck.** The parts differ from the working. The third write landed at 147.3, which is 3.6 us behind the landing of before in [rows 6] once that is moved by the 3.2 us of the projection; 1.2 was forecast. The eight issues took 5.2 us and the landing 2.4, 7.7 together for 9.4. The two errors nearly cancel in the stand, 5.0 for 4.4. The low clock behind it cost 1.4 and not 2.7, which cancels that in turn; 0.3 us is a wait of PE for DVE's copy at 147.35. A second gate, DVE's copy behind the third write, stood in the shadow of the first and wasn't seen; x2 uncovered it. The zeroing of the array cost nothing that shows. The bounds don't follow from the working: with the spread twice as long the stand alone is 13.8 us, so with its second price the loss is 16.5 and not 14; and it is nothing as soon as the spread lands by 153.1, not 151.

**Part 4, the projection (2.7 forecast): right in its mechanism.** The first product started at 21.19 (21.4 forecast), the eighth piece's rounding at 19.75, done by 20.4 (20.8). x6 shows that the piece gates, and prices the gate at 4.3 to 5.4 us. The gain is 3.2 us in one pair of profiles, 1.8 on their averages, 2.2 by z3's ratio; more can't be told.

**Rivals.** A (the spread is hidden) is what z1 does, and does not happen by itself. B falls with x8. C, a leak of DVE's work, is not seen: turns are 1.30 shorter, and in the whole run PE waits for a low part of the fold once, for 0.2 us, as before. D falls with x9: even sixteen DMAs were laid out in 12.2 us.

**The signs named.** Turns 61.57 (61.5 named); one stand of 5.0 us near 160 with a low clock behind it; 21.19; a gap between the last halves, 3.1 us and not 2. All four came.

By the table: the forecast's 15.6, less 4.9 of the last turn, less 1.1 of the turns, plus 0.5 of the projection, less 0.1 of turn 0, is 10.0 us, for 10.6 by the medians. The range held because it was wide enough for a miss of 5 us in one place.

## What to carry to other kernels

Where PE sets the time, price each new wait of its by the gap and by the stretch at the low clock behind it: here 3.1 us of standing cost 4.7 to 6.2 us, 2.3 cost 3.7 and 5.0 cost 6.4. A change inside a loop has edges: the turn that is written apart and the code ahead of the first turn took back 12 of 20 us, and both were mended by moving a step past work that nobody waits for, turn 0 with a semaphore more. Cut traces at fixed points before believing a total: in x1, x3 and x4 the stretch that the edit changes moved by 6.0, 1.9 and 1.9 us, and the total by 1.6, 15.4 and 4.2. But take a stretch from more than one profile: the same code took 72.0 to 73.9 us to the heads.

## What was not expected of the hardware

- Two stands of PE of 5.1 and 4.1 us without a releaser in x3, with 50 packets on the instruction queue for 42, gone with 47 more instructions at the start; they came with about 12 us in the median of six runs. That code loading stalls PE is a reading that fits; no row here shows it, and which address or length brings it on stays open.
- DVE beside POOL's subtractions: 64 columns took 1.05 and 1.24 us for 0.20 and 0.28, 512 columns 1.77 for 0.68 (x1's row at 1119.46, with POOL idle). The Trainium skill, page "SBUF — State Buffer", section Who interferes with whom, says that a DVE instruction with two SBUF inputs and a GpSimd instruction that reads SBUF exclude each other for the whole length of the one that came first, and that a copy or cast of DVE in a mode of two ports excludes GpSimd in the same way. The rows agree: L814 and L822 have two such inputs; L812 is a cast, whose mode no row shows. In the same profile an operation with two SBUF inputs (L461) took 1.16 us beside POOL's work, which ended at 1115.9, and 0.68 behind it, while a copy from PSUM beside it kept its 0.68:

```profile
1112.97 0.68 DVE L797 COPY x_mix<-s_ps 128x512 f32<-128x512 f32 x1
1113.57 1.16 DVE L461 TENSOR_TENSOR w_cT_lo<-e_wk,w_cT_hi 128x512 fp32r<-128x512 f32 x1
...
1116.95 0.68 DVE L461 TENSOR_TENSOR w_space_lo<-e_wk,w_space_hi 128x512 fp32r<-128x512 f32 x1
```
- The 64 short products of a half took 6.14 us in the last turn, with the granted clock at 0.50 for the first 4 us, and 3.65 at 1.00 in the loop. In the stretch at 0.50 (1125 to 1129) 37 were done, 0.11 us each for 0.057.
